# Inputs of two attention layers transposed ahead of their loops, and the second layer's queries and keys projected ahead

## The reference

```python
x = layernorm(x + attn0(x))      # q, v with a low-rank addition; all 256 tokens see each other
x = layernorm(x + experts(x))    # an expert is used only if few enough tokens chose it
x = layernorm(x + attn1(x))      # rotary positions on q and k, causal mask
x = layernorm(x + spline_ffn(x))

# attn:    qkv = x @ w_qkv;  softmax(q @ k.T * scale) @ v;  @ w_proj
# rotary:  q = q * cos + rotate_half(q) * sin   (k alike)
# experts: probs = softmax(x @ gate_w.T); top 2 of 8; counts = tokens per expert
#          keep = counts <= cap   (1.25 * tokens / 8)
#          contribution of the experts kept, times probs
# layernorm(x) = (x - mean) / sqrt(var + 1e-5)
```

## Time and profile before

| | |
|---|---|
| device time, three runs | 1359.0, 1361.35, 1361.97 us; median 1361.35 |
| the profiled execution | 1361.33 us, its span 1359.6 us |
| preparation | 0 to 22.1 us |
| first attention layer | 22.1 to 541.8 |
| expert stage | 541.8 to 591.3 |
| second attention layer | 591.3 to 1132.8 |
| spline_ffn | 1132.8 to 1359.6 |
| busy over the span | PE 80%, DVE 76%, ACT 61%, POOL 43% |

### The profile page before, as it was taken

How to read it: one execution, slowest core, us unless ns; L and a number is a source line. 1 busy time by engine, 2 the same in 40 slices (tenths; PEclk the granted TensorE clock), 3 DMA queues, 4 the chain that set the end, 5 groups by cost and what they waited for, 6 DMA issues and landing times. The chain is left out here.

```text
span 1359.6 us, 36441 instructions
## 1 busy us (share of the span) xinstructions
PE 1081.3 (80%) x11411; PEld 799.5 (59%) x11411; DVE 1029.6 (76%) x2823; ACT 835.7 (61%) x1904; POOL 582.8 (43%) x696
## 2 busy tenths in 40 slices
PE   2699999999999996516999999999999996501330
PEld 1366666666666663314888888888888873201220
DVE  3578888888888883824787788877888763698885
ACT  1267777777777774552666776767767664401675
POOL 3234434444444432434555555555555506000776
PEclk9799999999999998756999999999999998855555
DMA  2655555565556540305444554444554412100011
GB/s 57 151 122 136 131 139 128 133 140 131 136 135 137 135 100 10 115 29 134 120 119 121 119 123 120 116 121 119 124 119 120 115 35 82 43 0 0 24 47 54
DMA packets 122613, 137.33 MB, mean 101 GB/s; under 512 B 12562, under 2 KB 110258, under 8 KB 113330
## 3 DMA queue, kind: packets, MB, share of 16 engines
q1 hardware_dynamic: 121506, 136.50, 40.6%
q10 hardware_dynamic: 1040, 0.00, 0.0%
HBM read 85.03 MB, written 37.75 MB: 90 GB/s over the span
## 5 line engine op out<-in xcount | busy, mean ns | idle before, releaser
L376 DVE TENSOR_REDUCE attn_negmax<-attn_row_ps 128x2 f32<-128x512 f32 (+1 forms) x1024 | 597.8, 618 | 151.4 <-PE attn_row_ps L558 136.4
L317 ACT ACTIVATE attn_probs<-attn_col_ps 128x512 f32<-128x512 f32 (+1 forms) x1024 | 534.9, 546 | 111.8 <-PE attn_col_ps L580 106.5
L558 PE MATMUL attn_row_ps<-k_st,q_st 72*128 72x256 bf16 (+1 forms) x2048 | 370.3, 263 | 14.9 <-DMA k_st<-attn_scratch 13.9
L580 PE MATMUL attn_col_ps<-q_st,k_st 74*128 74x256 bf16 (+1 forms) x2048 | 369.8, 262 | 2.6 <-ACT attn_probs L317 2.0
L597 PE MATMUL attn_out_ps<-attn_probs,v_sb 128*32 128x256 f32 (+1 forms) x4096 | 230.4, 358 | 0.7 <-ACT attn_probs L317 0.7
L580 PEld LDWEIGHTS attn_col_ps<-q_st,k_st 74*128 74x128 bf16 x2048 | 184.3, 99 | 73.9 <-ACT attn_probs L317 23.2
L558 PEld LDWEIGHTS attn_row_ps<-k_st,q_st 72*128 72x128 bf16 x2048 | 201.9, 99 | 41.3 <-issue 15.3
L597 PEld LDWEIGHTS attn_out_ps<-attn_probs,v_sb 128*32 128x32 f32 x4096 | 123.3, 110 | 71.2 <-issue 21.3
L554 PE MATMUL attn_row_ps<-mask_qk,ident_h 128*128 128x256 bf16 x512 | 141.5, 276 | 19.1 <-DMA k_st<-attn_scratch 18.0
L576 PE MATMUL attn_col_ps<-mask_kq,ident_h 128*128 128x256 bf16 x512 | 141.3, 276 | 1.2 <-ACT attn_probs L317 1.0
L289 POOL TENSOR_SCALAR attn_var<-attn_mv 128x2 f32<-128x2 f32 x64 | 14.3, 223 | 265.8 <-DVE attn_mv L439 265.8
(11 more groups left out here) (230 smaller groups left out, 1689.0 us busy)
## 6 DMA issues: line engine op xcount, KB each, us to landing
q_st<-attn_scratch SPq DMA_DIRECT2D x192, 192.0 KB
k_st<-attn_scratch SPq DMA_DIRECT2D x192, 192.0 KB
attn_scratch<-attn_parts SPq DMA_DIRECT2D x64, 384.0 KB, 2.8
attn_scratch<-attn_parts SPq DMA_DIRECT2D x64, 128.0 KB, 2.9
x_in<-in_L_attn_x_dram SPq DMA_DIRECT2D x32, 128.0 KB, 2.6
x_all<-in_L_attn_x_dram SPq DMA_DIRECT2D x32, 128.0 KB, 7.0
moe_xs<-x_all SPq DMA_DIRECT2D x8, 512.0 KB, 2.9
x_in<-x_mid SPq DMA_DIRECT2D x32, 128.0 KB, 2.4
```

The costliest lines, as they stand in the source:

```text
L317: nc.scalar.activation(probs_of(st, 3, u)[:, j, 0:W], col_ps[:, n % 2, 0:W], ACT.Exp, scale=scale).then_inc(probs_kept, 1)
L376: nc.vector.tensor_reduce(negmax[:, t, 2 * p:2 * p + 2], row_ps[:, row_bank(st, u), 0:2 * keys].rearrange("p (a k) -> p a k", a=2), AX_X, ...
L558: last = nc.tensor.matmul(bank[:, a * keys:(a + 1) * keys], q_st[0:KROWS, sl, h, t * P:(t + 1) * P], k_st[0:KROWS, sl, h, 0:keys], start=n ...
L580: last = nc.tensor.matmul(bank[:, t * N:(t + 1) * N - first], k_st[0:rows, sl, h, t * P:(t + 1) * P], q_st[0:rows, sl, h, first:N], start= ...
```

## The change

The first layer: x is loaded once, in four pieces, into x_all; PE transposes it in sixteen groups of four tiles in the first steps (`x_front`: one ahead of step 0, two after it, ten after step 1, three after step 2), ACT copies the result into xT_all, for which x_mid's memory is used. In each step SP copies one batch of it to xT, for the product with the v weights; q and k are projected from xT_all directly. The 19 loads of spline tables go from SP's queue to ACT's. POOL computes, behind its layer norm, the second layer norm as well: since the first norm leaves mean 0 and variance var/(var+eps), r = 1/sqrt(var * rstd^2 + eps), and x_mid = x_all * r.

The expert stage: mean, variance, copies and the final layer norm are gone; the tiles of x_mid are transposed into the second layer's xT_all (x_all's memory), and the logits are divided by r before the routing. The routing runs in two halves of 32 tiles, the first beside the groups.

The second layer: all 32 projections of q and k are computed ahead, two matmuls and one ACT copy each (three copies each for the first three batches): 20 before step 0, 12 in step 2. ACT's queue stores them to DRAM, four batches a transfer; in each step SP loads the next batch's, also with halves exchanged, and POOL waits for that load. v is evicted after n = 5 instead of 4.

```diff
-AT = {"attn0": dict(act_xT=0, act_mT1=1, act_qk=(2, 4), ...
+AT = {"attn0": dict(act_mT1=1, act_qk=(2, 4), ...
-                    pe_xT=0, pe_mT1=2, pe_qk=2, ...
+                    pe_mT1=2, pe_qk=1, ...
...
+X_CHUNKS = ((0, 2), (2, 8), (8, 20), (20, 32))
+X_FRONTS = {-1: range(0, 1), 0: range(1, 3), 1: range(3, 13), 2: range(13, B // 2)}
+FRONT_GROUP = 4
+FRONT_EARLY = 20
...
# sync
-                sp.dma_start(x_in[:, st.slot(lag), :, :], src).then_inc(x_loaded[st.slot(lag)], 16)
+            def load_xT(st):
+                if st.has(3):
+                    sp.wait_ge(v_ready, st.seq(3, c=1))
+                ...
+                sp.dma_start(xT[:, st.slot(0), :], xT_all[:, bass.ds(st.seq(0), 1), :]...)
+            def load_qk(st):
+                sp.wait_ge(rest_kept, st.seq(2, c=1))
+                ...
+                sp.dma_start(qk[:, sl, :, :]..., of).then_inc(qk_loaded[sl], 16)
+                for to, of_row in ((0, P // 2), (P // 2, 0)):
+                    sp.dma_start(q_half[to:to + P // 2, sl, :, :]..., of[of_row:of_row + P // 2, :])...
# gpsimd
-                    pool.wait_ge(qk_kept, st.seq(0, QKOPS, QKOPS))
+                    if not fronted:
+                        pool.wait_ge(qk_kept, st.seq(0, QKOPS, QKOPS))
+                    elif st.loop or st.off >= SLOTS:
+                        pool.wait_ge(qk_loaded[st.slot(0)], st.turn(0, 16 * QK_LOADS, -16 * QK_LOADS))
...
+                        nc.gpsimd.tensor_tensor(square[:, :], rstd[:, :], rstd[:, :], ALU.mult)...
+                        nc.gpsimd.tensor_tensor(square[:, :], square[:, :], mv[:, :, 1], ALU.mult)...
+                        nc.gpsimd.tensor_scalar(square[:, :], square[:, :], EPS, 0.0, ALU.add, ALU.add)...
+                        nc.gpsimd.tensor_tensor(r_mid, square[:, :], mem["minus_half"][:, 0:TB], ALU.pow)...
+                        nc.gpsimd.tensor_tensor(mem["x_mid"][...], x_all[...], r_mid..., ALU.mult)...
# tensor
+            def front(b):
+                if b >= 2:
+                    pe.wait_ge(front_kept, kept_by(b - 2))
+                for s in range(2):
+                    last = nc.tensor.matmul(col_ps[:, b % 2, s * N:(s + 1) * N], wqk[:, s, :], xT_all[:, b, :], ...)
+                last.then_inc(front_ready, 1)
             def step(st):
                 for n in range(H):
+                    if fronted and not st.loop and st.off == 2 and FRONT_EARLY + n < B:
+                        front(FRONT_EARLY + n)
...
-                    if n == at["pe_xT"] and st.has(0):
-                        transpose_x(st)
...
-                    if n == at["pe_qk"] and st.has(0):
+                    if not fronted and n == at["pe_qk"] and st.has(0):
                         project_qk(st)
...
# expert stage, vector
-                groups(dve, step)
-                dve.wait_ge(logits_kept, GROUPS)
+                nc.vector.reciprocal(r_inv[:, :], r_mid[:, :]).then_inc(mean_kept, 1)
+                route(0)
+                route(1)
...
-                with dve.Fori(LN_SPLIT, GROUPS) as i:
-                    for t in range(GT):
-                        nc.vector.tensor_scalar(x_mid..., x_all..., mean[:, tile], rstd[:, tile], ...)
# prepare
-            load_spline(sp, mem, w)
+            for n in range(1, len(X_CHUNKS)):
+                load_x(n)
+        @block.scalar
+        def _(act):
+            act.wait_ge(zeroed, 9)
+            load_spline(act, mem, w)
```

More of the change, by code:

```diff
@@ L245, in step @@
             def step(st):
-                if st.has(4) and x_dram is not None:
+                if st.has(4) and not fronted:
                     wait(pool, y_kept, st.seq(4))
-                    pool.wait_ge(x_old_loaded[st.slot(4)], st.turn(4))
+                    if not st.loop and st.off == 4:
+                        for loaded in mem["x_loaded"]:
+                            pool.wait_ge(loaded, 16)
                     apart(pool, mem)
@@ L331, in step @@
                     for s in range(2):
-                        if n == at["act_qk"][s] and st.has(0):
+                        if not fronted and n == at["act_qk"][s] and st.has(0):
                             if s == 0:
@@ L362, in step @@
                             .then_inc(mT_kept, 1)
+                if not fronted and not st.loop:
+                    for g in X_FRONTS.get(st.off, ()):
+                        x_front(g)
+            if fronted:
+                for b in range(FRONT_EARLY):
+                    front(b)
+            else:
+                for g in X_FRONTS[-1]:
+                    x_front(g)
             pipeline(act, step)
@@ L640, with groups @@
 GROUPS = TILES // GT
-LN_SPLIT = 6
+HALF = TILES // 2
 MT = 4
-def groups(eng, step):
-    pipeline(eng, step, 2, 4, GROUPS, 0)
+def groups(step):
+    for n in range(GROUPS + 3):
+        step(Step(0, n, 2, GROUPS))
 def moe(nc, mem, w):
-    x_all, x_mid, ident = mem["x_all"], mem["x_mid"], mem["ident"]
+    x_all, x_mid, r_mid, ident = (mem[k] for k in ("x_all", "x_mid", "r_mid", "ident"))
+    xT_all = mem["xT_all"]["attn1"]
+    xT_flat = xT_all[:, :, :].rearrange("p b n -> p (b n)")
     with ExitStack() as ctx:
@@ L809, in step @@
                         last.then_inc(logits_ready, 1)
-                groups(pe, step)
-                pe.wait_ge(routed, COUNTED)
-                nc.tensor.matmul(g_ps[:, 0, 0:E], ones[:, :], counts[:, :], start=True, stop=True)\
-                    .then_inc(counts_ready, 1)
+                groups(step)
+                for half in range(2):
+                    pe.wait_ge(routed, COUNTED * (half + 1))
+                    last = nc.tensor.matmul(g_ps[:, 0, 0:E], ones[:, :], counts[:, half, :], start=half == 0,
+                                            stop=half == 1)
+                last.then_inc(counts_ready, 1)
             @block.scalar
             def _(act):
-                act.wait_ge(consts, E + 3)
+                act.wait_ge(consts, E + 2)
                 act.dma_start(gate_T[:, 0:E], w["L0_ffn_gate_w"].rearrange("e c -> c e"),
```

402 lines of the change are left out of this document (232 added, 170 removed).

## The result

| | before | after |
|---|---|---|
| median of the runs | 1360.88 us (4 runs) | 1416.97 us (4 runs, 1410.58 to 1421.48) |
| ratio, 95% interval | | 1.041 (1.0361 to 1.0459) |
| profiled execution, its span | 1361.33, 1359.6 | 1410.58, 1408.9 |

1362 us was forecast, in a range of 1326 to 1398.

What follows compares the result with a forecast made beforehand. PE was taken to set the step in both attention layers, DVE the expert stage. Terms of -25.2 us and +26 for the second layer's held norm gave +0.8: 1362 us, range 1326 to 1398 (its own bounds 1350 to 1374).

Steps and rivals of the forecast that it cites:

- The hold of the norm: Second layer: DVE's two norm instructions wait for POOL's sine and cosine products, 2.52 us instead of 0.60.
- D: Second layer: the extra time of DVE's norm in a step when POOL's products hold it, forecast 1.92 us.
- (1): Second layer: only the norm's first instruction waits, for the sine product; step 15.36, total 1336 us; chance 0.14.
- (2): Second layer: the norm starts before POOL's products and does not wait; step 14.43, total 1311 us; chance 0.13.
- (3): Second layer: the norm passes only with the cosine product and the sum; step 17.77, total 1401 us; chance 0.13.
- The second layer's step: A cycle through DVE's norm and first maximum sets 14.43 us; the held norm makes it 16.35, +26 us over 27 steps.
- a lower clock when PE waits 2 us of 16: One example of something slower not foreseen, in the second layer; chance 0.07 for all such cases, no size given.
- The first layer's steps: Two transposes leave PE in each step, 0.22 us saved in each of 29 steps, -6.4 us.
- not shorter than 14.6: Sign that the prediction's frame is wrong: the first layer's step fails to get below 14.6 us; 14.5 was expected.
- The second layer's fill: Projections computed ahead add PE work, but early steps lose other work; net -3 us, bounds -8 and +8.
- The start: Spline loads move to ACT, so the first layer's block opens at about 15.4 instead of 22.1 us, -6.7 us.
- the expert stage: DVE's statistics and final layer norm go, routing runs in two halves; 35.4 instead of 49.5 us, -14.1 us.

Runs made afterwards that it cites:

- x1_wait: Changed kernel; in the second layer POOL waits, after the reciprocal root, for DVE's layer norm before the next sine product: 1361.42 us, ratio 1.0006.
- x3_fill: Changed kernel; in the second layer PE computes the projection of v four times more before the fourth head's rows, results unused: 1394.21 us, ratio 1.0239.
- x2_qk2: Changed kernel with the first layer's projection of q and k put back behind the transposed maxima: 1404.72 us, ratio 1.0311.
- x11_start: Changed kernel; both layers' norm on POOL, projection loads behind maxima, first layer's q/k projection put back, last two x loads issued in first layer's block: 1302.83 us.
- x9: Changed kernel with only SP's three loads of projections moved behind the transfer of the first half of the maxima: 1414.3 us, ratio 1.0402.
- x8: Kernel before with five more DVE reductions, results unused, ahead of the second layer's norm: 1384.05 us, ratio 1.0148.

## Why the prediction was wrong

- **The hold of the norm (right).** D = 1.92 was forecast and 1.91 measured (2.51 - 0.60); rivals (1), (2) and (3) are out, and x1_wait shows that it is POOL's doing.
- **The second layer's step (wrong, and the largest part of the miss).** The step 14.43 + 1.92 = 16.35 holds for the steps at full clock (16.22 in x3_fill). What failed is what it leaves out: PE's wait of 2.3 us in each step was priced at its length alone. The granted clock fell behind it in every second step or so, 28 us more. It stood only in the 0.07 for "a lower clock when PE waits 2 us of 16", and no row of before shows PE waiting 2 us in a steady step, so that its cost could not be read off and a bound was due: the expert stage has a row with the clock down (0.67).
- **The first layer's steps (wrong).** By its own sign ("not shorter than 14.6") the prediction fails here: the step is 15.15. "29 x 0.22 = -6.4 us" counted the instructions that left PE and passed over the one that moved. The order of L607 and L594 held ACT's copy and cost 12.3 us (x2_qk2); the 0.22 itself was hidden work and gave 0. The diff of the table and the order of ACT's queue showed both.
- **The second layer's fill (wrong).** -3 was forecast and +6.7 came. In the fill PE is busy 65.8 of 81.3 us, before 47.1 of 74.6, so PE has 18.7 us more busy time and 12.0 less idle time, while the DMA share rose from 0.42 to 0.71. PE still waits 7.5 us for the first stacks (18.0 before), 4.0 for exponentials and 2.1 for the maxima's transfer. How much of the +6.7 is work and how much DMA was not separated, and stays open.
- **The start.** SP's issues of the three x loads were priced at about 2 us in all and took 7.95. With the two large ones issued later, x11_start opens at 15.05; 15.4 was forecast.
- **Two numbers of the working.** The bounds of the terms, added up, give 1350 to 1383, not 1374; and the sum is slower than before from D = 1.87 up, not 1.95. Neither changes the verdict.
- **Right:** the expert stage (-14.1, -14.8) and POOL's tail (+2.3, +1.9).
- **The next bound (missed).** 512 KB of loads stand ahead of the maxima in SP's queue. In the changed kernel the norm hides it (x9); it would have spoiled rival (2) too: its 1311 us assumed a step of 14.43, and with the norm free the step is 15.21 (x1_wait).

## What to carry to other kernels

When a wait is taken away, look at what it kept apart: POOL's wait for ACT was what let DVE's norm through. Price a wait of PE by what the clock does behind it as well, and look for a piece of idle work or, better, for an order without the wait. In a list written out by hand, an operation moved by one place is to be followed on the engines that wait for its neighbours; and of small transfers on the critical path see that no large ones stand ahead of them in the queue.

## What was not expected of the hardware

- More work gave less time: four idle projections a step (x3_fill), -22.8 us, by keeping PE at its upper clock. Waits of 2.3 us were followed, in about every second step, by some 3.5 us at 0.52; waits of 0.75 (x8, clock 1.00) and of 1.1 on average (x1_wait, clock 0.99 to 1.00) hardly or never.
- A DMA issue on SP's queue can take long when large loads stand ahead of it: 0.43 and 0.41 us for the loads of 256 and 768 KB, 1.79 and 4.92 for two of 1.5 MB each (0.89 and 3.22 in x11_start, where they are issued some 4 us later). What holds the second of two equal ones longer was not tried.
